# Reading back sorted rows in a graph kernel on one core: 1024 rows to a transfer, column lookups ahead of the one-hot, and a later clear of the sums

## What is computed

```python
h_j = x[col]                                   # col = dst, row = src
c_e = comps[edge_type]                         # 4 coefficients per edge
hj_b = c_e[:, :, None] * h_j[:, None, :]
msg = jnp.einsum('ebd,bdf->ef', hj_b, bases)
msg = msg * alpha[edge_type] * norm[:, None]
out = jax.ops.segment_sum(msg, row, num_segments=n)
```

## Time and profile before

| what | us |
|---|---|
| median of 3 runs (8995.79 to 9006.86) | 9003.98 |
| the profiled execution's own time | 8996.33 |
| its span in the trace | 8994.6 |
| relation phase, from the memset of the sums to the last sum | 4144.9 to 6742.9 |
| PE busy in the whole span | 6838.9 (76%) |
| POOL busy | 5985.1 (67%) |
| DVE busy | 5025.3 (56%) |
| ACT busy | 1795.2 (20%) |

### The profile page before, as it was taken

The page is one execution under the profiler, slowest core; times in us unless marked ns, Lnnn a source line. Parts: engine busy times, 40 slices in busy tenths (PEclk is TensorE's granted clock), DMA queues, the critical chain, the costliest instruction groups (busy, mean ns, idle before and its releaser), DMA issues. The chain is left out here.

```text
span 8994.6 us, 165062 instructions
## 1 busy us (share of the span) xinstructions
PE 6838.9 (76%) x39312; PEld 5322.2 (59%) x39312; DVE 5025.3 (56%) x13644; ACT 1795.2 (20%) x5149; POOL 5985.1 (67%) x6303
## 2 busy tenths in 40 slices
PE   2766667676777777776777788886773899999997
PEld 2666566565555454454555577775662677777776
DVE  6445545455666666664222256654445567677666
ACT  1111111111222121222222222220002122222221
POOL 3777777776777777775777777772001777777774
PEclk7555555555767777777777799996665555555555
DMA  6344444443333333332222255553444333333332
GB/s 195 122 142 132 137 142 127 142 133 96 88 85 90 85 89 89 85 90 81 82 84 83 83 152 162 164 155 99 109 107 128 91 92 92 90 92 90 93 91 63
DMA packets 886407, 979.31 MB, mean 109 GB/s; under 512 B 139646, under 2 KB 711216, under 8 KB 886063
## 3 DMA queue, kind: packets, MB, share of 16 engines
q1 hardware_dynamic: 592437, 482.50, 18.3%
q0 software_dynamic: 200960, 418.41, 17.4%
q10 hardware_dynamic: 92794, 76.22, 2.8%
HBM read 649.26 MB, written 333.71 MB: 109 GB/s over the span
## 5 line engine op out<-in xcount | busy, mean ns | idle before, releaser
L2160 POOL DMA_INDIRECT soft_rows<-proj,soft_slot x1564 | 1501.1, 960 | 1269.5 <-ACT soft_slot L2181 823.6
L755 POOL DMA_INDIRECT L_rows<-H,L_slot x1568 | 1487.5, 949 | 613.3 <-issue 601.4
L1575 POOL DMA_INDIRECT sorted<-msg_out,msg_idx x1564 | 1497.9, 958 | 494.3 <-issue 451.4
L1029 POOL DMA_INDIRECT L_rows<-H,L_slot x1568 | 1484.6, 947 | 479.6 <-issue 437.7
L893 PE MATMUL L_sum<-L_onehot,L_rows 128*128 128x64 f32 x3136 | 705.9, 400 | 590.6 <-DMA L_rows<-H,L_slot 564.0
L1664 PEld LDWEIGHTS msg_ps_msg<-msg_hb,msg_lhs 128*128 128x128 f32 x6272 | 944.2, 238 | 194.1 <-issue 193.5
L893 PEld LDWEIGHTS L_sum<-L_onehot,L_rows 128*128 128x128 f32 x3136 | 648.6, 306 | 653.2 <-issue 497.5
L1619 DVE SCALAR_TENSOR_TENSOR msg_lhs<-msg_dst_sp,msg_node,msg_ps_c 128x512 f32<-128x512 f32 x784 | 550.6, 744 | 864.2 <-ACT msg_dst_sp L1588 805.0
L1664 PE MATMUL msg_ps_msg<-msg_hb,msg_lhs 128*128 128x128 f32 x6272 | 1031.7, 332 | 0.3 <-DVE msg_lhs L1619 0.3
L1673 PE MATMUL msg_ps_sum<-msg_back,msg_lo_hot 128*128 128x128 f32 x3936 | 699.0, 339 | 180.2 <-DVE sums_r L1639 154.1
L2289 PE MATMUL soft_ps_sum<-soft_onehot,soft_x 128*128 128x64 f32 x3136 | 752.2, 422 | 85.1 <-DVE sums_b L2406 82.4
(11 more groups left out here) (394 smaller groups left out, 11283.3 us busy)
## 6 DMA issues: line engine op xcount, KB each, us to landing
sorted<-L_zeros SPq DMA_DIRECT2D x394, 330.0 KB
msg_back<-sorted SPq DMA_DIRECT2D x492, 264.0 KB
L_rows<-H,L_slot POOLq DMA_INDIRECT x3136
msg_hb<-HB SPq DMA_DIRECT2D x392, 128.0 KB
soft_at_in<-in_edge_attr_dram SPq DMA_DIRECT2D x195, 256.0 KB
HB<-L_prod ACTq DMA_DIRECT2D x49, 512.0 KB, 3.0
sorted<-msg_out,msg_idx POOLq DMA_INDIRECT x1564
soft_rows<-proj,soft_slot POOLq DMA_INDIRECT x1564
```

The source lines that it names most:

```text
L755: pool.indirect_dma_start(rows[:, k, j, :], None, t["H0"], bass.IndirectOffsetOnAxis(ap=slot[:, k, j:j + 1], axis=0)).then_inc(gathered[k] ...
L1029: pool.indirect_dma_start(rows[:, k, j, :], None, t["H1"], bass.IndirectOffsetOnAxis(ap=slot[:, k, j:j + 1], axis=0)).then_inc(gathered[k] ...
L1575: pool.indirect_dma_start(t["sorted"], bass.IndirectOffsetOnAxis(ap=idx[:, s, j:j + 1], axis=0), out[:, s, j, :], None, **({} if w is None ...
L2160: pool.indirect_dma_start(rows[:, s % SC, j, :], None, t["proj"], bass.IndirectOffsetOnAxis(ap=slot[:, s, j:j + 1], axis=0)).then_inc(gath ...
```

## The change

Three things. The transfers of `return_rows` take two blocks (1024 rows) each, into three buffers of twice the size; one is issued at every other block and waits until the block five before its first one is totalled. The two loads from `unit_col` are no longer inside `gain` but in a step of their own, `find_columns`, which stands ahead of `find_own` of the block two behind. The memset of the sums goes from the start of the phase to the call of `after` behind the first 52 turns, ahead of group 208.

```diff
-        back, lo_hot = sb("back", [P, R3, 4, WR]), sb("lo_hot", [P, R3, 4, P])
+        back, lo_hot = sb("back", [P, R3, 8, WR]), sb("lo_hot", [P, R3, 4, P])
...
             def return_rows(i, q):
-                b = i * BQ + q
-                sp.wait_ge(totalled, b + 1)
-                sp.nop(nofuse=True)
-                sp.dma_start(back[:, q % R3, :, :], tiles_of(t["sorted"], b * 4, 4)).then_inc(returned[q % R3], 16)
+                if q % 2 == 0:
+                    b = i * BQ + q
+                    sp.wait_ge(totalled, b + 2)
+                    sp.nop(nofuse=True)
+                    sp.dma_start(back[:, q // 2, :, :], tiles_of(t["sorted"], b * 4, 8)).then_inc(returned[q // 2], 16)
...
             link = Link(v, prep)
-            link(v.memset(acc, 0.0), False)
             link(v.tensor_copy(ps_columns[:, 0:P], t["iota"][:, :]), False)
...
+            cols = {}
+
+            def clear_sums(turns, k):
+                if k < 2:
+                    v.memset(acc, 0.0).then_inc(prep, 1)
+                    v.wait_ge(prep, link.n + 1)
...
             def find_own(i, q):
                 b = i * BQ + q
-                v.wait_ge(returned[q % R3], (i * (BQ // R3) + q // R3) * 16 + 16)
-                v.wait_ge(totalled, b + 1)
-                own, columns = bcast(back[:, q % R3, :, F], 2, P), bcast(ps_columns[:, 0:P], 1, 4)
+                v.wait_ge(returned[q // 2], i * 16 + 16)
+                v.wait_ge(totalled, b + 1 + BQ - R3)
+                own, columns = bcast(back[:, q // 2, q % 2 * 4:q % 2 * 4 + 4, F], 2, P), bcast(ps_columns[:, 0:P], 1, 4)
...
+            def find_columns(i, q):
+                b = i * BQ + q
+                cols[q] = [v.value_load(t["unit_col"][0:1, ds(b * 2 + u, 1)], min_val=0, max_val=(S.NT + 2) * P) for u in range(2)]
+
             def gain(i, q):
                 b = i * BQ + q
-                for u in range(2):
-                    at = v.value_load(t["unit_col"][0:1, ds(b * 2 + u, 1)], min_val=0, max_val=(S.NT + 2) * P)
-                    v.wait_ge(totalled, b + 1 + R3)
+                for u, at in enumerate(cols.pop(q)):
+                    v.wait_ge(totalled, b + 1 + BQ)
                     v.wait_ge(gained, b * 2 + u + 2 * R2)
                     v.tensor_tensor(acc[:, ds(at, P)], acc[:, ds(at, P)], ps_sum[q % R2][:, u * P:(u + 1) * P], ALU.add).then_inc(gained, 1)
-            with_blocks(v, S, t, [(0, make_lhs)], [(0, find_own), (2, gain)])
+            with_blocks(v, S, t, [(0, make_lhs)], [(2, find_columns), (0, find_own), (2, gain)], after=clear_sums)
...
-            pe.sem_inc(totalled, R3)
+            pe.sem_inc(totalled, BQ)
...
-                    mm = pe.matmul(ps_sum[q % R2][:, k // 2 * P:(k // 2 + 1) * P], lo_hot[:, q % R3, k, :], back[:, q % R3, k, 0:F],
+                    mm = pe.matmul(ps_sum[q % R2][:, k // 2 * P:(k // 2 + 1) * P], lo_hot[:, q % R3, k, :], back[:, q // 2, q % 2 * 4 + k, 0:F],
                                    start=(k % 2 == 0), stop=(k % 2 == 1))
```

## The result

The changed kernel takes 9033.5 us (median of 6 runs), the kernel before 9001.3 us (median of 6). The ratio is 1.0036, 95% interval 1.0025 to 1.0047: slower by 0.36%, 32 us, clearly beyond the 0.2% that can be told from nothing. The profiled execution of the changed kernel is the longest of its six, 9049.4 us, span 9047.6; the other five lie between 9032.9 and 9036.1. It differs from the profiled execution of before by more than the change: everything that GpSimd paces runs 0.2% slower in it, ahead of the change too (1.2535 against 1.2510 us from one indirect DMA to the next, before 4140 us).

A forecast was written before the change was run, and what follows sets the result against it. GpSimd was taken to bound up to 6143 us, then VectorE's steps, mostly lengthened by late transfers. Terms +0.9 + 68.1 - 10.8 = +58.2 us gave 9062 us on the median's scale, range 9005 to 9105 (8 in 10).

The forecast's parts named there:

- Transfers: Block transfers of 1024 rows: they cease to bound the blocks' own stretch; the exposed first one costs +0.9 us.
- SyncE's earlier requests: Beside the scatters: rows and HB asked for about 5 us earlier, TensorE's 95 us of waits nearly go; 0 us.
- Lookups: Blocks' own stretch: both lookups paid in the open, step 2.75 us in place of 2.465, +68.1 us over 239 steps.
- The forecast's sign of 1.65 us of idle time: Profile after, blocks' own stretch: about 1.65 us of VectorE idle laid to issue in each step.
- The cover beside the scatters: Beside the scatters, 252 blocks: lookups cost nothing, four groups taking VectorE 17.5 us against 20.2 us of scatters.
- The memset: Phase start and group 208: first scatter 10.8 us earlier, the stall covered by 11.4 us of copied groups; -10.8 us.
- Rival A: Blocks' own stretch: sequencer passes the second sum's wait, lookups hidden, step 2.08 us, -102 us, 8902 us; chance 0.12.
- Rival B: Blocks' own stretch: second adjacent lookup hides its 0.30 us load, step 2.45, -13.5 us, 8990 us; chance 0.09.
- Rival C: Scatter stretch: reserve of copied groups runs out, memset move gives nothing, +69 us, 9073 us; chance 0.07.

The follow-up runs named there:

- the memset alone: The kernel before with only the memset moved behind group 208: 8997.5 us against 9003.0, ratio 0.9995.
- the lookups put back: The changed kernel with the two lookups again inside the sums, transfers and memset as changed: 8913.4 us against 9003.0 for the kernel before, ratio 0.9902.

## Why the prediction was right, point by point

The direction, the place and the mechanism held; the range of 9005 to 9105 us holds 9033.5. The size was too large: +58 us forecast, +32 measured, and nearly all of the miss is one term, the step.

1. *Transfers.* +0.9 us for the longer first one: +0.8. That they cease to bound: no wait behind the first. That SyncE's earlier requests remove TensorE's waits for HB rows: gone.
2. *Lookups.* This is the term that was mis-sized: a step of 2.75 us, +68.1 us; measured 2.662, +47.0. By its own parts: one-hot to first sum 0.60, measured 0.60. First to second sum 0.49, measured 0.41 (the 0.49 was read beside a group, where one more sequencer instruction stands between the two). Two lookups and the dispatch of the one-hot 2 x 0.73 + 0.20 = 1.66, measured 6406.45 - 6404.87 = 1.58: the 0.20 was the distance of two VectorE instructions, of which the dispatch is only a part. Left out was the loop's return, which every sixth step pays: it is 3.13 us in place of 2.58, 0.09 us per step. So 0.08 and 0.08 too much and 0.09 too little, which partly cancel by luck; of the 21 us these make some 18, and the other 3 are the first six steps, which stand ahead of the loop and are shorter. The forecast's sign of 1.65 us of idle time was a distance from start to start; the second sum's own 0.29 us lie in it, so 1.3 us of idle time is what it amounts to.
3. *The cover beside the scatters.* The lookups cost nothing there, and the reserve grew again, from 3.8 us at group 208 to 11.4 at group 220.
4. *The memset.* 10.8 us forecast, 11.0 measured. It doesn't hold up the scatters, which keep their 1.26 us beside it, as the 1.25 us in the earlier trace rows. The lock of which the Trainium skill warns (SBUF — State Buffer, "SBUF: two separate sides") is that of an instruction in a two-port mode; this memset shows none, and in what mode it runs no trace says.

Rival A needed the sequencer to pass the second sum's wait. It doesn't: the lookups start at 6404.9, 0.03 us behind the second sum's start at 6404.87, and in no step ahead of it. Line 1649 from 6403.8 to 6406.4 us has the instruction in which the sequencer waits:

```profile
L1649 DVEq FUSED_REGOPS  x2: 46/46/46, 6404.0 to 6404.8; - x2
```

The second of these register instructions carries the wait for `gained` in the trace and starts at 6404.77, just after the first sum has ended (6404.73). The Trainium skill (Perfetto Trace Analysis, "DVE / Act Engine Instruction") has an instruction wait in a queue while the sequencer goes on, and this doesn't speak against it: here the wait is not on the sum but on a register instruction of the sequencer ahead of it.

Rival B (an overlap of two lookups) is excluded by the two loads 0.7 us apart. Rival C is what happens without the transfers, as the memset alone shows: the first scatter 10.5 us sooner, and no time gained.

What the prediction didn't see is how much was there to be had: the same edit without its lookup half is worth 90 us.

## What to carry to other kernels

Where an engine's instructions are short, add up its sequencer's program as well: a lookup of 0.7 us is free only beside an instruction of its engine that lasts as long, so register work belongs behind the longest instruction that needs none of it, and a "prefetch" that moves it out from there makes it dearer. When a loop through a DMA and a program of one sequencer are nearly as long (2.4 and 2.2 us here), taking one off shows only the other, and both have to be priced before. A reserve that an engine has built up pays for a stall if it lasts to the end: here it did where it was refilled (11.4 us again after 12 groups), and where it was being drained already the moved memset gained nothing.

## What the runs showed of the hardware that was not expected

The check of a loaded value costs nearly as much as its load: 0.27 us a lookup (0.54 a step) beside 0.30 for the load itself, and taking it away was worth 119 us of 9016 (ratio 0.9902 with it, 0.9770 without).

TensorE's granted clock followed the spacing of its work, at the same 1920 instructions: 0.51 where a step was 2.66 us (eight passes 2.08 us, then idle 0.5 us), 0.66 at 2.465, 0.80 at 2.16, 0.99 at 1.615 (eight passes 1.16 us, then idle 0.35). 0.5 is the lower of its two levels, 1.2 GHz, and 0.66 and 0.80 are means of times spent at either. The clock did not set these steps: with the lookups put back the middle steps of a set take 2.07 to 2.09 us at both levels. In the changed kernel it stayed at the lower level nearly throughout, although from the second set of passes on TensorE was never idle for more than 1.6 us at a time. I had left open which level the shortest step would get; it got the upper one, and at the lower one eight passes alone would have taken 2.08 us. That the spacing brings the level is what the order of these kernels suggests; no run changed the spacing alone.
